# A two-layer graph network on one core: the first table and the tails in two-tile units, and 20 rows a round fetched by SP and ACT

## What is computed

```python
def conv(x, src, dst):                       # layer 0
    e = relu((x[dst] - x[src]) @ theta_w.T + theta_b + x[src] @ phi_w.T + phi_b)
    return where(isfinite(m := segment_max(e, dst)), m, 0)
def gnn(x, he, src, dst):                    # layer 1
    hv = x @ W_in + b_in
    for W, b in ((W_u0, b_u0), (W_u1, b_u1)):
        m = relu(concat([hv[src], he]) @ W + b)
        hv = where(has_in, segment_max(m, dst) + hv, hv)
    return relu(hv @ W_ro + b_ro)
x = layernorm(x + conv(x, src, dst))
x = layernorm(x + gnn(x, he, src, dst))
```

## Time and profile before

| what | value |
|---|---|
| median of 3 runs | 3896.59 us (3896.26 to 3897.47) |
| profiled execution, its own time | 3892.11 us |
| its span | 3890.5 us |
| mean granted clock of TensorE | 0.766 |
| busy: POOL, PE, DVE, ACT | 64%, 56%, 37%, 4% |
| DMA engines, mean over the span | 196 GB/s |

### The profile page before, as it was taken

One profiled execution on the slowest core, in us unless ns is written; L12 is line 12 of the kernel. 1 busy time (PEld: TensorE's weight loads), 2 busy tenths in 40 slices (PEclk: granted clock), 3 DMA queues, 4 the chain that ended last, 5 costly groups with the idle time before them and its releaser, 6 DMA issues.

```text
span 3890.5 us, 19202 instructions
## 1 busy us (share of the span) xinstructions
PE 2167.8 (56%) x5026; PEld 1019.8 (26%) x5026; DVE 1450.7 (37%) x3561; ACT 148.4 (4%) x352; POOL 2486.2 (64%) x2518
## 2 busy tenths in 40 slices
PE   5112211112221747777777777764776777777766
PEld 4011111111111513333333333351232223222225
DVE  2345454455544413333333333321333333333335
ACT  1000000000000200000000000030000000000002
POOL 1766666666664666666666666376666666666636
PEclk8555555555555868888988898896888988888878
DMA  5545555555555946666666666564665656666656
GB/s 181 172 162 198 195 195 187 169 197 199 195 198 167 288 137 213 221 213 206 217 223 207 205 216 223 173 131 138 212 216 198 214 201 216 206 210 213 206 177 157
DMA packets 260441, 763.80 MB, mean 196 GB/s; under 512 B 52675, under 2 KB 118317, under 8 KB 222702
## 3 DMA queue, kind: packets, MB, share of 16 engines
q0 software_dynamic: 135360, 334.92, 30.3%
q1 hardware_dynamic: 82638, 363.42, 24.3%
q10 hardware_dynamic: 42336, 64.24, 5.5%
HBM read 415.19 MB, written 347.19 MB: 196 GB/s over the span
## 4 chain that ended last, share of the span: by engine, by line
PE 35%; DVE 23%; another core or an unknown queue 21%; issue 11%; POOL 5%; DMA 3%; SPq 1%; DVEq 1%; ACT 0%; POOLq 0%; ACTq 0%
DVE hist L338 18%; PE edge_ps L708 16%; PE edge_ps L705 16%; POOL hv_sb L546 4%; PE edge_ps L662 1%; DVE junk L275 1%; DMA x1T<-hist 1%; DVE junk L272 1%; POOL gath L520 1%; PE side_ps L662 1%; SPq L424 1%; DVEq L336 1%; DVE above L256 0%; DVE counts L277 0%
## 5 line engine op out<-in xcount | busy, mean ns | idle before, releaser
L520 POOL DMA_INDIRECT gath<-table,src_sb x2352 | 2248.1, 956 | 1145.9 <-issue 633.5
L338 DVE SCALAR_TENSOR_TENSOR hist<-hist,keep,edge_ps 128x256 f32<-128x256 f32 x1568 | 753.6, 481 | 1545.2 <-remote 676.4
L705 PE MATMUL edge_ps<-w_e,he_sb 128*128 128x512 f32 x1568 | 934.0, 680 | 595.4 <-DVE hist L338 381.7
L708 PE MATMUL edge_ps<-gath,ident 128*128 128x512 f32 x1568 | 907.7, 664 | 19.3 <-DMA gath<-table,src_sb 17.3
L671 PE MATMUL side_ps<-dst_f,onehot 128*128 128x512 f32 x200 | 147.8, 893 | 909.3 <-DVE onehot L258 806.1
L705 PEld LDWEIGHTS edge_ps<-w_e,he_sb 128*128 128x128 f32 x1568 | 303.2, 210 | 1103.3 <-issue 697.5
L338 DVE SCALAR_TENSOR_TENSOR hist<-hist,lift,gath 128x256 f32<-128x256 f32 x784 | 380.0, 485 | 367.3 <-DVE hist L338 117.4
L708 PEld LDWEIGHTS edge_ps<-gath,ident 128*128 128x128 f32 x1568 | 333.3, 213 | 462.1 <-issue 437.7
L671 PEld LDWEIGHTS side_ps<-dst_f,onehot 128*128 128x128 f32 x200 | 58.2, 321 | 986.7 <-DVE onehot L258 825.6
L546 POOL DMA_INDIRECT hv_sb<-runs,end_zero x98 | 151.2, 1543 | 32.7 <-issue 29.3
L588 ACT COPY hv_sb<-side_ps 128x256 f32<-128x256 f32 x98 | 36.5, 372 | 2244.1 <-issue 822.5
(11 more groups left out here) (104 smaller groups left out, 812.8 us busy)
## 6 DMA issues: line engine op xcount, KB each, us to landing
runs<-hist SPq DMA_DIRECT2D x294, 1024.0 KB
he_sb<-in_he ACTq DMA_DIRECT2D x196, 256.0 KB
gath<-table,src_sb POOLq DMA_INDIRECT x2352
table<-hist SPq DMA_DIRECT2D x63, 256.0 KB
gath<-in_xT POOLq DMA_DIRECT2D x7, 896.0 KB, 10.9
back_T<-in_xT ACTq DMA_DIRECT2D x49, 128.0 KB
gath<-in_x SPq DMA_DIRECT2D x7, 896.0 KB, 13.6
x<-gath SPq DMA_DIRECT2D x7, 896.0 KB
```

The source lines that it names most:

```text
L338: V.scalar_tensor_tensor(hist[:, s % H, :], hist[:, (s - 1) % H, :], fresh[:, t:t + 1], edges, ALU.add if r == 0 else ALU.mult, ALU.max).t ...
L520: pool.indirect_dma_start(gath[:, s % G, :], None, tables[r], bass.IndirectOffsetOnAxis(src_sb[:, t:t + 1], 0)).then_inc(gathered[s % G // ...
L705: T.matmul(bank, he_sb[:, c % NHE, at:at + P], w_e[r - 1][:, :], start=True, stop=False)
L708: T.matmul(bank, ident[:, :], gath[:, at:at + 2, :].rearrange("p s f -> p (s f)"), start=False, stop=True).then_inc(pair_summed, 1)
```

## The change

- **Rounds.** Steps 736 to 755 of each round are no longer gathered by POOL. SP (12 steps) and ACT (8 steps) fetch their rows one by one: for a partition the node numbers are loaded into registers and each register addresses a transfer of one row of 1 KB. SP's are spread ahead of the stores of chunks 0 to 89 of 98, ACT's over turns 0 to 44 of 49. The rings become G = 20 (plus 20 rows for the fetched steps) and H = 24. `keep` is gone: all rounds add `lift`. x now stays on the chip (`x_sb`), loaded in round 0.
- **First table.** Units of two tiles, four PSUM banks, four staging buffers with a semaphore each; SP issues the edge loads only, the weights are issued by ACT after the table, and the first gather no longer waits for the biases. Products of weights and bias splitting are done in turns 1 and 2 of round 0.
- **Tails.** The maxima are gathered without add into a ring of eight units; the base term comes from back products, in round 2 too (`w_in_n1` in round 1, `w_in_ro` and `w_ro` with two left sides in round 2). Normalisation runs by units, with the scaling on ACT. ACT applies the relu when it copies turned tiles.
- `find_ends` has 10 in place of 12 steps, since one row number serves all rounds.

The core of the diff:

```diff
+AHEAD, BY_ACT, BY_SP = 736, 8, 12
+EXT = BY_ACT + BY_SP
+GATHERS = STEPS - EXT
-G, H = 48, 40
+G, H = 20, 24
-QSTEPS = 12
+QSTEPS = 10
+XT_BUFS, ROW_BUFS, UNIT_BUFS = 12, 8, 4
...
+        def parts_at(n, turns):
+            return range(P * n // turns, P * (n + 1) // turns) if n < turns else ()
+        def fetch_rows(eng, regs, r, p, first, n):
+            eng.load(regs, src_sb[p:p + 1, AHEAD + first:AHEAD + first + n])
+            for k in range(n):
+                node = eng.snap(regs[k], min_val=0, max_val=NPAD - 1)
+                eng.dma_start(ext[p:p + 1, first + k, :], tables[r][bass.ds(node, 1), :]
+                              ).then_inc(row_fetched[(first + k) // 2], 16)
...
             def store_runs(r):
...
                 for c in range(CHUNKS):
+                    if r == 0 and 0 <= c - FIRST_X_CHUNK < TILES:
...
+                        sp.dma_start(x_sb[:, i, :], a["x"][i * P:(i + 1) * P, :]).then_inc(x_loaded, 16)
+                    for p in parts_at(c, AHEAD // SC - 2):
+                        fetch_rows(sp, sp_regs, r, p, BY_ACT, BY_SP)
                     n = r * CHUNKS + c
                     sp.wait_ge(state_done, (n + 1) * SC)
...
             def feed_edges(r):
...
                 for i in range(TURNS):
+                    for p in parts_at(i, AHEAD // BODY - 1):
+                        fetch_rows(act, act_regs, r, p, 0, BY_ACT)
...
             def gather_edges(r):
                 for t in range(STEPS):
+                    if is_ahead(t):
+                        continue
+                    j = nth_gather(r, t)
+                    if j % 2 == 0 and j >= G:
+                        freed = step_of(j - G)
+                        if freed < STEPS:
+                            pool.wait_ge(state_done, freed + 2)
+                        else:
+                            pool.wait_ge(pair_summed, freed // 2 - PAIRS + 1)
...
+            def gather_maxima(r):
+                pool.wait_ge(fix_written, 16 * (r + 1))
...
+                for u in range(NU):
+                    lo, hi = unit(u)
+                    if u >= ROW_BUFS and r == 0:
+                        pool.wait_ge(normed, u - ROW_BUFS + 1)
+                    elif u >= ROW_BUFS:
+                        pool.wait_ge(tile_turned, r * NU + u - ROW_BUFS + 1)
+                    for k in range(hi - lo):
+                        pool.indirect_dma_start(rows(u)[:, k, :], None, runs[0:SPARE, :],
+                                                bass.IndirectOffsetOnAxis(end_row[:, lo + k:lo + k + 1], 0)
+                                                ).then_inc(row_landed[u % ROW_BUFS], 16)
...
                 if r == 0:
-                    pool.wait_ge(w_loaded, 16 * len(weight_loads))
-                    pool.wait_ge(setup_step, setup_at["all"])
-                    pool.wait_ge(none_written, 16)
+                    pool.wait_ge(edges_loaded, 16 * len(edge_loads))
...
+            def norm_units(n, to_sum, add):
+                for u in range(NU + 1):
...
+                    if u < NU:
+                        y = flat(to_sum(u))
+                        add(u, y).then_inc(summed, 1)
+                    if u > 0:
+                        dve.wait_ge(std_ready, m)
+                        V.reciprocal(rstd[:, before, :], std[:, before, :]).then_inc(rstd_ready, 1)
+                    if u < NU:
+                        dve.wait_ge(summed, m + 1)
+                        V.scalar_tensor_tensor(y, y, 0.0, flat(x_sb[:, lo:hi, :]), ALU.max, ALU.add).then_inc(resid_added, 1)
...
+            def normalise(n, u, to, of):
...
+                for k in range(hi - lo):
+                    last = A.activation(to[:, k, :], of[:, k, :], ACT.Identity, bias=shift[:, at, k:k + 1],
+                                        scale=rstd[:, at, k:k + 1])
+                last.then_inc(normed, 1)
...
+                linear(back_ps, lefts, ((w_theta,), (w_in_n1,), (w_in_ro, w_ro))[r],
+                       (CONV, NEXT1, OUT)[r]).then_inc(back_product, 1)
```

More of the change, by code:

```diff
@@ L23 @@
 TILES = -(-NODES // P)
[L24 to L25 removed]
 NPAD = TILES * P
+NU = -(-TILES // 2)
 ROUNDS = 3
@@ new lines, in rows_there, with landed, uses @@
+        def rows_there(r, t):
+            if is_ahead(t):
+                return row_fetched[(t - AHEAD) // 2], 2 * 16 * P * (r + 1)
+            j = nth_gather(r, t)
+            return gathered[j % G // 2], 2 * 16 * (j // G + 1)
+        def landed(r, u):
+            here = [16 * (hi - lo) for lo, hi in map(unit, range(u % ROW_BUFS, NU, ROW_BUFS))]
+            return r * sum(here) + sum(here[:u // ROW_BUFS + 1])
+        def uses(n, u):
+            return n * len(range(u % UNIT_BUFS, NU, UNIT_BUFS)) + u // UNIT_BUFS
@@ new lines, in add_base @@
+            def add_base(u, y):
+                lo, hi = unit(u)
+                dve.wait_ge(product, 3 * NU + u + 1)
+                if u >= UNIT_BUFS:
+                    dve.wait_ge(normed, NU + u - UNIT_BUFS + 1)
+                return V.tensor_tensor(y, product_ps(u), flat(hv_sb[:, lo:hi, :]), ALU.add)
+            edge_maxima(0)
+            join_runs(0)
+            dve.wait_ge(x_loaded, 16 * TILES)
+            dve.wait_ge(back_kept, TILES)
+            norm_units(0, rows, add_product)
@@ new lines, in _ @@
+            for u in range(NU):
+                write_table(0, u)
+            sp.wait_ge(setup_step, setup_at["none row"])
+            sp.dma_start(runs[NONE:NONE + 1, :], none_row).then_inc(none_written, 16)
+            store_runs(0)
+            for u in range(NU + 1):
+                if u < NU:
+                    write_turned(0, u)
+                if u > 0:
+                    write_table(1, u - 1)
+            store_runs(1)
+            for u in range(NU + 1):
+                if u < NU:
+                    write_turned(1, u)
+                if u > 0:
+                    write_table(2, u - 1)
@@ L499, in _ @@
+            store_runs(2)
+            for u in range(NU):
+                write_out(u)
+            for written, n in all_written(out_written, 1):
+                sp.wait_ge(written, n)
         @block.gpsimd
@@ new lines, in messages, with turn @@
+                    there, count = rows_there(r, 2 * p)
+                    pe.wait_ge(there, count)
+                    T.matmul(bank, ident[:, :], flat(edge_rows(r, 2 * p, 2)), start=False, stop=True).then_inc(pair_summed, 1)
+                    if p % (BODY // 2) == BODY // 4 - 1:
+                        back(r * TILES + p // (BODY // 2))
+            def turn(r, u, of):
+                if r * NU + u >= 4:
+                    pe.wait_ge(turned_out, r * NU + u - 3)
+                lo, hi = unit(u)
+                for k in range(hi - lo):
+                    for h in range(KH):
+                        last = T.transpose(turned_ps(u)[:, k * D + h * P:k * D + (h + 1) * P],
+                                           of[:, k, h * P:(h + 1) * P], ident[:, :])
+                last.then_inc(tile_turned, 1)
```

766 lines of the change are left out of this document (370 added, 396 removed).

## The result

The changed kernel takes 4997.8 us (median of 4 runs, 4979.9 to 5000.4) beside 3896.4 for the kernel before (4 runs): a ratio of **1.282 [1.279, 1.285]**. The forecast was 3717. Its profiled execution is 4979.9 us with a span of 4977.7.

What follows compares the result with a forecast made beforehand. No engine was full; POOL's gathers and the consumer were taken to hold each other up in the rounds. The terms -33 + 11 - 75 - 5 - 82 + 4 = -180 gave 3717 us against the median of 3896.6, range 3630 to 3900.

Steps and rivals of the forecast that it cites:

- (h): Single-row fetches on SP and ACT in the rounds: 0.55 us a row against room for 0.64, so cost nothing.
- Rival 1: SP's queue becomes the bound in the rounds, late stores holding DVE, PE and POOL; 4263 us at 0.76 a row; chance 0.18.
- (e): Histories cut from 40 to 24 steps: a store must land 16 steps after its last; cost nothing, cover 16 us.
- (a): First table: first gather at 57 us instead of 90.1, a gain of 33 us, bounds 16 to 40.
- (b): Weight products and bias splitting now on DVE inside round 0: cost 11 us, bounds 0 and 22.
- (d): find_ends loses two small DVE operations, 50 times by about 0.1 us: gain 5 us, bounds 0 and 10.
- (g): Base term from a back product with two feeds in round 2 too, on PE: cost 4 us, bounds 0 and 15.
- (c): POOL issues 20 gathers fewer a round at 1.25 us each: 25 us a round, gain 75 in all.
- rival 2: The consumer alone bounds the rounds, so fewer gathers only lengthen POOL's waits and (c) is 0: 3792 us; chance 0.17.
- (f): Tails: plain gathers of maxima and normalising on ACT gain 27, 25 and 30 us, together 82, between 40 and 120.
- rival 5: In the tails the gather of maxima without its add still takes 1.84 us: 3769 us; chance 0.02.
- Rival 4: Tails keep their pace because DVE or PE's low clock takes over from POOL; (f) falls to 20, 3779 us; chance 0.05.

Runs made afterwards that it cites:

- e1: Changed kernel with no rows fetched by SP or ACT, POOL gathering all 784 steps a round, rings of 20 and 24 kept; held condition: 3802 us.
- e8: Changed kernel with SP fetching six steps row by row in place of twelve and ACT none, 778 gathers a round; free condition: 3316 us.
- e16: Changed kernel with SP fetching six steps and ACT four, 774 gathers a round; free condition: 3303.2 us, 0.961 of the kernel before.
- e5: Changed kernel with the 20 late steps fetched by nobody (work left out), 764 gathers a round; free condition: 35 us less than e8.
- e18: Changed kernel with SP fetching six steps and ACT six, 772 gathers a round; held condition: 4211.5 us, 1.081 of the kernel before.
- e10: The changed kernel itself run once more, in the free condition: 3431.2 us beside 3437.0 for the kernel before, 0.998.

## Why the prediction was wrong, step by step

**(h) failed.** "I bound the price of a row from 0.38 (nothing for them) to 0.76 (as much again) and take 0.55." Free, it is 0.57 to 0.63, not far off. Held, as in the runs of the result, it is 0.90, outside the bounds, and "Cost nothing" became the 1196 us between e1 and the changed kernel. Rival 1 named the path, SP's late stores, with too low a price and a chance of 0.18. The 0.90 comes from the round by its formula; the trace's own count, 0.93, bears it out. The bounds were made of rows of SP's queue at 2 to 3 and 74 us, where POOL does not gather. Yet the prediction's own first part said that the consumer is slow only while POOL issues. I applied that to DVE and PE and not to the queue onto which the change moved 1536 rows, three instructions each, every one of which can be held, although SP's 39 late stores were in the trace before. The room of 0.64 us a row was also too wide: it came from a round of 1107, the others' average pace. Free, nobody's 965 leaves 0.56, so even there the forecast's 180 us came to 6.

**(e)'s cover** of 16 us was named with the condition under which it goes ("gone once SP issues a store that much late"), and it went: DVE's longest wait for a store is 25.7 us.

**(a)** First gather at 55.6, forecast 57. Right. **(b), (d), (g)** are inside the rounds and not told apart there. With no rows (e1) the three rounds took 42 us less in all than before. I had +10 for these three, and (c) does not apply to e1, so that is 52 better than I said. The ring of 40 gives back 32 of it; the other 20 were not told apart.

**(c)** 75 us were not seen held, since SP took the bound. Free, going from six to ten steps (e8 to e16) gave 12 us for 12 gathers, 1.0 each, and from e8 to e5 35 us for 42, 0.84 each: under the 1.25, and far from rival 2's 0.

**(f) was too large**: 15 us for 82. The gather of maxima is plain as I said, 0.98 us on average in tail 0, so rival 5 was wrong. But POOL is not tail 0's pace. This is the chain in it, in order of time.

```profile
1631.87 1.10 ACT x_sb L705 x2
1633.02 1.12 PE side_ps L828 x4
1634.13 1.71 PE edge_ps L759 x4
1636.06 1.71 PE edge_ps L759 x4
1638.49 1.10 ACT x_sb L705 x2
...
1661.24 1.10 ACT x_sb L705 x2
1665.51 1.10 ACT x_sb L705 x2
1669.78 1.10 ACT x_sb L705 x2
```

A unit takes 6.6 us first and 4.27 from about 1645 on. ACT normalises, PE turns, ACT copies, PE multiplies, ACT copies again and only then normalises the next: I had added up 2.4 us of ACT's work a unit and set it beside POOL's, but in ACT's order it is a chain through PE. In the first stretch four matmuls of 256 columns take 1.71 us and later 0.87, which is the lower and the higher of the clock's two levels: the granted clock is 0.56 from 1631 to 1644 us and 1.00 from 1646 to 1710. Tails 1 and 2, forecast 96 and 103, are 109 and 117 held, at a granted clock of 0.77 and 0.81, and 91 and 94 free, at 0.85 and 0.89. Rival 4's size for (f), 20 us, was near, but not for its reason: it named DVE or PE's low clock as the new pace, and in tail 0 ACT's order sets 4.27 us a unit at the full clock too.

**Loads and contention.** The rows show a load of twelve registers on SP at a median of 1.89 us and of eight on ACT at 0.78, 0.16 and 0.10 a register. The Trainium skill's "Runtime: NRT & Kernel Launch", section "Instruction fetch mechanics", gives about 200 ns a register; the runs put SP's a fifth under it and ACT's at half, six on SP (e8, free) at 0.19, and e18's six, at 3.2 us, far over it. By the prediction's own sentence on that price, arithmetic above 0.06 us would make SP the bound; arithmetic and move are 0.14 even at their medians. The Trainium skill's "SBUF — State Buffer", section "Who interferes with whom", has transfers issued from SP and ACT contend with neither DVE nor GpSimd. Free, e10's trace agrees as far as POOL goes: beside 7680 such transfers its longest gap between gathers is 0.3 us. Held, SP's issue is what suffers beside POOL's gathers; the rule does not speak of instructions without a transfer, which suffer as well.

## What to carry to other kernels

Work moved to a queue is priced beside what runs next to it there, not in a quiet stretch; where a trace shows one engine slow only while another issues, take the same for the queue that is to get the work, and count the instructions a row, not the rows. A queue that carries stores or copies which others wait for has the room that the fastest pace of the others leaves it, not that of today's pace. What is worth keeping of this change is the first table, the tails and the ring of 20 with POOL gathering all 784 steps: 0.976 held, with no rows on a queue whose stores or copies others wait for (it was not run free); six and four steps by SP and ACT gave 0.961 free, but six and six cost 8% held.

## What the runs showed of the hardware

- One program ran in two conditions, 3437 to 3440 and 3887 to 3897 us for the kernel before, 3431 and 4998 for the changed one, and one chip showed both at different times. Executions of a kernel taken together agreed within 1%. What makes the condition is open.
- In the held one, instructions on SP's and ACT's queues begin late beside POOL's gathers by steps of 0.7 us, register moves too: 30% of SP's in the changed kernel, 0.7% in the free one, none of those by more than 0.4 us. Stores are late too (39 of 294 in the kernel before, none in e5), and DVE's steps stand for an unnamed releaser (745 us in e1, none in e5).
- A single row of 1 KB at a register's address costs its queue 0.42 us with nothing held, 0.28 of it the transfer, and loading its register adds 0.10 (ACT, eight at once) to 0.19 (SP, six at once).
